# Linear attention and FFN on one core: reciprocals of the denominators taken by rows, split in two parts, and spread by products with a 0/1 matrix

## The reference

```python
q, k, v = phi(proj(Wq, bq)), phi(proj(Wk, bk)), proj(Wv, bv)     # phi = elu + 1
# chunks of 128 tokens, state (S, z) carried from one to the next
num  = mask(q k^T) v + q S
kcum = cumsum(k) + z
den  = sum(q * kcum, over the 16 features of a head)             # one number per token and head
out  = num / den
x = x + (out @ Wo.T + bo)
h = layernorm(x) * gamma + beta
x = x + 0.5 * (silu(h @ w1 + b1) @ w2 + b2)
```

## Time and profile before

| what | value |
|---|---|
| median of 3 runs | 1517.52 us (1516.9 to 1517.61) |
| the profiled execution's own time | 1522.6 us |
| its span, first to last instruction | 1520.8 us |
| mean granted TensorE clock | 0.991 |
| PE busy | 1493.2 us, 98% |
| DVE busy | 1283.5 us, 84% |
| ACT busy | 1129.7 us, 74% |
| POOL busy | 680.7 us, 45% |

### The profile page before, as it was taken

One profiled execution on the slowest core, in us unless ns is written; L12 is line 12 of the kernel. 1 busy time (PEld: TensorE's weight loads), 2 busy tenths in 40 slices (PEclk: granted clock), 3 DMA queues, 4 the chain that ended last, 5 costly groups with the idle time before them and its releaser, 6 DMA issues.

```text
span 1520.8 us, 40737 instructions
## 1 busy us (share of the span) xinstructions
PE 1493.2 (98%) x14874; PEld 1311.2 (86%) x14874; DVE 1283.5 (84%) x2587; ACT 1129.7 (74%) x1917; POOL 680.7 (45%) x469
## 2 busy tenths in 40 slices
PE   7799999999999999999999999999999999999998
PEld 6588889888888888888888888888888888988887
DVE  6788888888888888888888888888888888888875
ACT  3487777887777887777887777887777877777863
POOL 3244344544344544345444445443445443445444
PEclk8899999999999999999999999999999999999999
DMA  7846765556765556764557765557654557755450
GB/s 198 194 118 150 179 148 149 137 131 152 179 158 131 131 133 164 179 156 133 131 122 175 179 133 143 137 125 179 179 138 138 133 129 179 174 134 141 117 127 28
DMA packets 153944, 222.96 MB, mean 147 GB/s; under 512 B 20032, under 2 KB 71488, under 8 KB 153920
## 3 DMA queue, kind: packets, MB, share of 16 engines
q1 hardware_dynamic: 152560, 222.63, 61.0%
q10 hardware_dynamic: 1360, 0.01, 0.1%
HBM read 138.69 MB, written 83.89 MB: 146 GB/s over the span
## 4 chain that ended last, share of the span: by engine, by line
PE 93%; DVE 2%; DMA 2%; POOL 1%; issue 1%; SPq 0%; ACT 0%; POOLq 0%; DVEq 0%
PE ring L342 35%; PE num L532 8%; PE ring L420 8%; PE sc L490 7%; PE ring L421 7%; PE sc L342 6%; PE num L499 4%; PE num L342 3%; PE state_acc L342 3%; PE ring L372 3%; PE state_acc L490 2%; PE ring L566 2%; PE state_acc L513 2%; PE num L421 1%; PE num L420 1%; PE num L372 1%
## 5 line engine op out<-in xcount | busy, mean ns | idle before, releaser
L1137 POOL TENSOR_TENSOR s_lo<-silu_f,s_hi 128x512 fp32r<-128x512 f32 x256 | 343.9, 1349 | 539.0 <-ACT s_hi L987 538.9
L342 PE MATMUL ring<-w_hi,s_hi 128*128 128x256 f32 x992 | 282.2, 284 | 0.0
L342 PE MATMUL ring<-w_lo,s_hi 128*128 128x256 f32 x992 | 278.9, 281 | 0.0
L342 PE MATMUL ring<-w_hi,s_lo 128*128 128x256 f32 x992 | 278.9, 281 | 0.0
L672 DVE TENSOR_TENSOR probs<-sc,causal 128x512 f32<-128x512 f32 x320 | 207.6, 681 | 16.1 <-PE sc L490 8.6
L342 PEld LDWEIGHTS ring<-w_hi,s_hi 128*128 128x128 f32 x992 | 187.8, 189 | 12.1 <-DVE phi_q L718 12.0
L1032 ACT ACTIVATE x_hat<-x,hn_add,ln_rstd 128x256 f32<-128x256 f32 x128 | 66.5, 590 | 174.6 <-DVE hn_add L860 174.6
L976 ACT ACTIVATE silu_f<-ring,bias,scale 128x512 f32<-128x512 f32 x217 | 167.5, 772 | 31.9 <-PE ring L421 23.5
L420 PE MATMUL ring<-gt_hi,w_q 128*128 128x512 f32 x441 | 190.5, 432 | 0.0
L342 PEld LDWEIGHTS ring<-w_hi,s_lo 128*128 128x128 f32 x992 | 188.0, 189 | 0.0
L342 PEld LDWEIGHTS ring<-w_lo,s_hi 128*128 128x128 f32 x992 | 187.9, 189 | 0.0
(11 more groups left out here) (204 smaller groups left out, 3946.2 us busy)
## 6 DMA issues: line engine op xcount, KB each, us to landing
k_stack<-k_rows SPq DMA_DIRECT2D x192, 256.0 KB, 4.1
q_stack<-q_rows SPq DMA_DIRECT2D x384, 128.0 KB, 6.2
k_rows<-silu_f SPq DMA_DIRECT2D x128, 256.0 KB, 2.6
q_rows<-probs SPq DMA_DIRECT2D x128, 256.0 KB, 2.5
x_in<-in_x SPq DMA_DIRECT2D x32, 512.0 KB, 8.4
xb<-in_x SPq DMA_DIRECT2D x32, 512.0 KB, 7.9
out<-clip SPq DMA_DIRECT2D x64, 256.0 KB, 7.5
silu_f<-in_q SPq DMA_DIRECT2D x2, 512.0 KB, 10.4
```

The lines of the kernel that those rows point to most:

```text
L342: last = e.matmul(target, a, b, start=(n == 0), stop=(n == 3 * len(pairs) - 1))
L1137: sl.done(e.tensor_tensor(s_lo[:, j, :], silu_f[:, j % SLOTS, :], s_hi[:, j, :].bitcast(F32), ALU.subtract))
```

## The change

The denominators are now laid out so that a row of `num[1]` holds one head of one chunk: `head_one` has two variants of 32 columns, and for each of the four 32-row groups two fp32 products of 128 columns (chunk 2*half and 2*half+1) are summed into it. Every denominator stands in two rows. There is no copy out and no transpose back: VectorE takes one reciprocal of 128x128 straight from PSUM. ScalarE makes from it, in four operations of 128x128 with a factor of 0 or 1 per row (`row_kind`), the rounded part and the full value, GpSimd subtracts them (128x256) so that one of the two rows holds the rounded reciprocal and the other the remainder, and TensorE multiplies these by a 0/1 matrix `spread`, two float32r products of 256 columns with 64 rows per half t, in place of the four transposes. `values(3)` now stands ahead of `spread_reciprocals(0)`. VectorE's `residual` moves from the start of the iteration to behind `attention(1)`. GpSimd builds `row_kind` and `spread` once, at the start.

```diff
-                        last = e.matmul(num[1][32 * g:32 * g + 32, 0:2 * P], head_one[:, :],
-                                        qk[:, t, 2 * P * half:2 * P * (half + 1)], start=True, stop=True,
-                                        skip_group_check=True)
+                        for q in range(2):
+                            c = 2 * half + q
+                            last = e.matmul(num[1][32 * g:32 * g + 32, 0:P], head_one[:, q, :],
+                                            qk[:, t, c * P:(c + 1) * P], start=(q == 0), stop=(q == 1),
+                                            skip_group_check=True)
                 den_pe.done(last)
 
-            def denominators_back():
-                w.need(den_sb, 0)
-                for x in range(2):
-                    last = e.transpose(num[1][:, (2 + x) * P:(3 + x) * P], den_rows[:, x * P:(x + 1) * P], ident[:, :])
-                den_tr.done(last)
-
             def spread_reciprocals(t):
-                w.need(rspread, 0)
+                w.need(rden_made, 0)
                 free_bank(w, f"rb{t}", present)
-                for c in range(C):
-                    last = e.transpose(ring_bank(f"rb{t}")[:, c * P:(c + 1) * P],
-                                       qk[:, t, c * P:(c + 1) * P], ident[:, :])
+                rows = slice(t * 2 * 32, (t + 1) * 2 * 32)
+                for half in range(2):
+                    last = e.matmul(ring_bank(f"rb{t}")[:, half * 2 * P:(half + 1) * 2 * P],
+                                    spread[rows, half, :], rden_parts[rows, :, :].rearrange("p q n -> p (q n)"), start=True, stop=True)
                 rb_pe.done(last)
@@ order on TensorE
             fc1(3)
-            denominators_back()
             scores(3)
...
             from_state(2)
+            values(3)
             spread_reciprocals(0)
-            values(3)
@@ VectorE
             def reciprocals():
-                w.need(den_tr, 0)
-                for t in range(T):
-                    last = e.reciprocal(rden_tok[:, t, :, :].rearrange("p (a x) h -> p a x h", a=2), den_tok(t))
-                rden.done(last)
+                w.need(den_pe, 0)
+                rden.done(e.reciprocal(rden_full[:, 0, :], num[1][:, 0:P]))
...
             if Fn:
-                residual()
                 ffn_input_lo()
...
             attention(1)
+            if Fn:
+                residual()
@@ ScalarE, in place of denominators_out and reciprocals_spread
+            def reciprocals_low():
+                w.need(rden, 0)
+                for q in range(2):
+                    e.activation(rden_parts[:, q, :], rden_full[:, 0, :], ACT.Copy, scale=row_kind[:, 2 + q, 0:1])
+                for q in (1, 0):
+                    last = e.activation(rden_full[:, q, :], rden_full[:, 0, :], ACT.Copy, scale=row_kind[:, q, 0:1])
+                rden_low.done(last)
@@ GpSimd, ahead of ffn_lo(3)
+            def reciprocal_parts():
+                w.need(rden_low, 0)
+                rden_made.done(e.tensor_tensor(rden_parts[:, :, :], rden_full[:, :, :], rden_parts[:, :, :].bitcast(F32), ALU.subtract))
@@ GpSimd, once, behind the memset of v_pad: 15 operations, the longest of them
+                for n in range(T * 32 // HT):
+                    t, d = divmod(n, 32 // HT)
+                    e.wait_ge(p_spread, P_KIND + n)
+                    e.affine_select(out=ones_at, in_=ones_at, compare_op=ALU.not_equal, fill=1.0, base=-(64 * t + HT * d),
+                                    pattern=[[-32, 2], [-1, HT], [0, HD]], channel_multiplier=1).then_inc(p_spread, 1)
```

More of the change, by code:

```diff
@@ L142, in build @@
         probs = [sb(f"probs{n}", [P, HT, P]) for n in range(2)]
-        den_rows = sb("den_rows", [P, 2 * P])
+        rden_full = sb("rden_full", [P, 2, P])
+        rden_parts = sb("rden_parts", [P, 2, P], F32R)
+        spread = sb("spread", [P, 2, P], F32R)
+        row_kind = sb("row_kind", [P, 4, 4])
         gt_hi, gt_lo = sb("gt_hi", [P, T, S], F32R), sb("gt_lo", [P, T, S], F32R)
@@ L282, in build @@
         Waiter.idle = sem("idle")
+        p_spread = sem("p_spread")
         p_const, p_bias, p_dma = sem("p_const"), sem("p_bias"), sem("p_dma")
@@ L784, in reciprocals @@
             def reciprocals():
-                w.need(den_tr, 0)
-                for t in range(T):
-                    last = e.reciprocal(rden_tok[:, t, :, :].rearrange("p (a x) h -> p a x h", a=2), den_tok(t))
-                rden.done(last)
+                w.need(den_pe, 0)
+                if not Fn:
+                    e.wait_ge(p_spread, P_SPREAD)
+                rden.done(e.reciprocal(rden_full[:, 0, :], num[1][:, 0:P]))
             def attention(t):
@@ L1046, in keys_out @@
                                         ring_bank(f"kt{n}")[:, :].rearrange("p (c d) -> p c d", c=2), ACT.Copy))
[L1048 to L1052, removed]
+            def reciprocals_low():
                 w.need(rden, 0)
-                rspread.done(e.activation(qk[:, :, :].rearrange("p t (c h x) -> p (t c h) x", c=C, x=HD),
-                                          rden_tok[:, :, :, :].rearrange("p t c h -> p (t c h)")[:, :, None]
-                                          .to_broadcast([P, U * HT, HD]), ACT.Copy))
+                if not Fn:
+                    e.wait_ge(p_spread, P_SPREAD)
+                for q in range(2):
[3 more added lines that the diff above has]
+                rden_low.done(last)
             def reciprocals_out(t):
@@ L1090, in ac_iteration @@
             if A:
-                reciprocals_spread()
+                reciprocals_low()
             ffn_scaled(4)
@@ L1141, in po_iteration @@
             for j in range(2, FT):
+                if A and j == 3:
+                    reciprocal_parts()
                 if A and j == FT - 2:
@@ L1235, in build @@
         V_W1, V_BIAS_O, V_BETA, V_W2, V_BIAS_2 = 3, 4, 5, 6, 7
-        CONSTS = 6 + 6 + 1 + 1
+        CONSTS = 6 + 8 + 1 + 1
         def stage_of(n):
@@ L1331, in _, with reciprocal_rows @@
             po_norm(e, Waiter(e, -1), 1)
+            def reciprocal_rows(e):
+                kinds = row_kind[:, :, :].rearrange("p (k q) g -> p k q g", k=2)
+                ones_at = rden_full[:, :, :].rearrange("p a (h x) -> p a h x", x=HD)
+                e.memset(row_kind[:, :, :], 1.0).then_inc(p_spread, 1)
+                e.memset(rden_full[:, :, :], 0.0).then_inc(p_spread, 1)
+                e.wait_ge(p_spread, 2)
+                e.affine_select(out=kinds, in_=kinds, compare_op=ALU.is_ge, fill=0.0, base=0,
+                                pattern=[[-HT, 2], [-2 * HT, 2], [-32, 4]], channel_multiplier=1).then_inc(p_spread, 1)
+                e.wait_ge(p_spread, 3)
+                e.affine_select(out=kinds, in_=kinds, compare_op=ALU.is_ge, fill=0.0, base=2 * HT - 1,
+                                pattern=[[0, 2], [2 * HT, 2], [32, 4]], channel_multiplier=-1).then_inc(p_spread, 1)
+                e.wait_ge(p_spread, 4)
+                e.tensor_tensor(row_kind[:, :, 0:2], row_kind[:, :, 0:2], row_kind[:, :, 2:4], ALU.add).then_inc(p_spread, 1)
+                e.wait_ge(p_spread, 5)
+                e.tensor_tensor(row_kind[:, :, 0:1], row_kind[:, :, 0:1], row_kind[:, :, 1:2], ALU.add).then_inc(p_spread, 1)
+                for n in range(T * 32 // HT):
[3 more added lines that the diff above has]
+                                    pattern=[[-32, 2], [-1, HT], [0, HD]], channel_multiplier=1).then_inc(p_spread, 1)
+                e.wait_ge(p_spread, P_SPREAD - 1)
+                e.tensor_tensor(spread[:, :, :], rden_full[:, :, :], rden_full[:, :, :], ALU.mult).then_inc(p_spread, 1)
             e.wait_ge(xhat.sem, xhat.value(0, 0))
             e.memset(v_pad[:, :, :, :, :], 0.0).then_inc(p_const, 1)
+            reciprocal_rows(e)
             po_iteration(e, -1, False, False, True, True)
```

20 lines of the change are left out of this document (11 added, 9 removed).

## The result

| | before | after |
|---|---|---|
| median | 1517.21 us (6 runs, 1514.79 to 1519.65) | 1526.87 us (6 runs, 1524.47 to 1530.74) |
| ratio | | 1.0070, 95% interval 1.0057 to 1.0082 |
| profiled execution: span | 1520.8 us | 1525.8 us |

What follows compares the result with a forecast made beforehand. TensorE was taken to bound the kernel (93% of the chain). Profiled: 1522.6 + 1.2 (0.04 us over 31 batches) + 0.5 at the start = 1524.3 us; median 1517.5 + 1.7, say 1519; range 1507 to 1530, forecast's own 1515 to 1524.

Steps and rivals of the forecast that it cites:

- the places of the ties: Between denominators and fc1(7), TensorE is tied to others at three places: fc1(3)'s weight load, mask(2) before scores(3), ffn_sum(6) before fc1(7).
- the hidden operand chain: Reciprocals through VectorE, ScalarE and GpSimd: operand ready at 734.8, needed by TensorE at 735.3, so hidden with 0.5 us of room.
- rival 2: Column groups of denominators fall in line instead of side by side: slower, 1526 to 1536 us, strict order 1546; chance 0.15.
- Two prices, 0.12 and 0.20 us, and a 64-row product switches the mode: On TensorE, 0.12 us into narrow products, 0.20 out; the 64-row spreads assumed to cost 0.20 in and 0.20 out.
- rival 1: The 64-row spreading products need no mode switch: 0.29 us a batch faster, 1509 us; chance 0.30.
- `denominators` side by side: Four 32-row groups still run in parallel on TensorE with 8 products of 128 columns: 0.44 against 0.44 us, no change.
- Rival 3: The spread's operand reaches TensorE late, after values(3): 0.25 us a batch, 1526 us; chance 0.05.
- The transposes' removal, 0.09: Dropping the two L558 transposes lets scores(3) stream earlier on TensorE, limited by mask(2): gain 0.09 us.
- Nearest is the middle ... 0.5 us, nothing changes: VectorE's one 128x128 reciprocal, between 0.24 and 0.96 us, taken as 0.5 against 0.48 before; at 0.96, 0.2 us a batch lost.
- The later one counts: 0.04 us later than before: Second half of fc1(7): VectorE's side ready at 740.66, TensorE's at 740.79, so 0.04 us a batch longer, +1.2 us over 31.
- Once, at the start, 0.5: Eight GpSimd selections of 128x256 beside VectorE's weight splits cost 0.5 us once, bounds 0 to 2.
- `residual` hidden by `phi_k`: Moved residual fills VectorE's idle 1.45 us before phi_k, ending 0.13 late, absorbed by phi_q's 0.49 of idle; decides over 2 us.

Runs made afterwards that it cites:

- e1: Changed kernel with the 0/1 spread matrix given all 128 rows (zeros outside the wanted token half); ratio 1.0006 to the kernel before.
- b_no_back: Kernel before without the two transposes that bring the denominators back, attention left undivided; ratio 0.9982 to the kernel before.
- e4: Changed kernel with the reciprocal taken of only 32 of the 128 columns (result partly wrong); ratio 1.0020 to the kernel before.
- e3: Changed kernel with only VectorE's residual moved back to the start of its iteration; ratio 1.0040 to the kernel before.
- e5: Changed kernel with VectorE's attention(0) moved behind ffn_sum(6); ratio 1.0072 to the kernel before.
- before_again: Kernel before, unedited, run again for a second trace; its execution took 1519.46 us, with batches of 45.64 us.
- e6: Changed kernel with the full-height (128-row) spread and attention(0) behind ffn_sum(6); ratio 1.0016 to the kernel before.
- e7: Changed kernel with full-height spread, attention(0) behind ffn_sum(6), and each half's second spreading product split into two of 128 columns; ratio 1.0043 to the kernel before.
- e9: Changed kernel with full-height spread, attention(0) behind mask(6), and shared buffers at the kernel before's SBUF addresses; ratio 1.0047 to the kernel before.
- b_attention_later: Kernel before with only attention(0) moved behind ffn_sum(6) on VectorE; ratio 1.0040 to the kernel before.
- the second comparison: The changed kernel, unedited, timed again beside the kernel before; ratio 1.0086 (1.0071 to 1.0101).

## Why the prediction was right and wrong

The prices of the switches, the places of the ties and the hidden operand chain were right. The forecast itself, 1.7 us slower with a range of its own of 1515 to 1524, was not: 9.7 us were lost. That 1526.9 lies in the stated range of 1507 to 1530 is luck, since the part above 1524 was put there for rival 2, which didn't come true.

- *Two prices, 0.12 and 0.20 us, and a 64-row product switches the mode* (forecast against rival 1): right. Both spreads show it, and e1, which differs in the height of the tile, gets 0.24 us back. Rival 1 is out.
- *`denominators` side by side* (against rival 2): right, 0.66 against 0.61 us. Rival 3 is out as well: 0.7 us of room.
- *The transposes' removal, 0.09*: right; `scores(3)` streams 0.11 us earlier in the batch than in before, of which 0.03 were there at `fc1(3)` already, and b_no_back has 0.09 at the end of the stretch.
- *"Nearest is the middle ... 0.5 us, nothing changes"*: the first step that failed. The reciprocal takes 0.87 us of VectorE's time, 0.39 more than the pair before; its length grows with its columns (348 ns for 32 in e4, 946 for 128). The free time that the prediction counted ahead of `fc1(4)`, some 0.3 us, was about right, and 0.39 is 0.1 more than that. It cost just the lead won at the transposes: `fc1(4)` streams 0.01 us later than in before, not 0.09 earlier. The prediction had 0.96 as upper bound, and 0.2 us a batch for it.
- *"The later one counts: 0.04 us later than before"*: the term that was mis-sized. TensorE's own side counted with that lead of 0.09. Without it the 0.04 are 0.13, and with the 0.07 of wait in `scores(6)` (e3, e5) they are 0.20. The traces show 0.20 and 0.19 in the median.
- *The long run of products*: not in the prediction at all. It took the "even distance" as given. 119.0 instead of 118.15 ns over 132 products is 0.11 us a batch, a third of the loss.
- *Once, at the start, 0.5*: the first key product starts at 14.31 us, in before_again at 13.69:
```profile
13.69 0.47 PE L342 MATMUL ring<-xt_hi,wk_hi 128*128 128x512 f32 x1 [1.81 <-DVE xt_lo L704]
```
```profile
14.31 0.47 PE L344 MATMUL ring<-xt_hi,wk_hi 128*128 128x512 f32 x1 [2.10 <-DVE xt_lo L703]
```
  All four traces without the change have 13.63 to 13.69, those with it 13.99 to 14.53. The eight selections aren't the cause: they begin at 14.08 on GpSimd, 0.6 us after VectorE began on that product's last operand. What is ahead are two more selections for `head_one`: GpSimd's first power of the norm starts at 8.16 instead of 7.84. That is half of the 0.6; the other half wasn't traced. By the first `fc2` the mean lies 2.5 us later (107.5 to 114.7 in ten traces with the change, 106.4 to 111.6 in four without), but this goes with TensorE's granted clock, whose mean over the first 106 us is 0.82 to 0.90. The three traces with the change that have 0.87 there (e4, e6, e7) reach the first `fc2` at 108.3 to 109.2, and before, with 0.87 as well, at 109.2; at 0.89 it is 107.5 in e9 and 106.6 in b_attention_later. So a loss of 2.5 us isn't shown. Whether the change alters the clock there is open.
- *`residual` hidden by `phi_k`*: right in its place (it ends as `phi_k` starts), but not free: e3 has 0.06 us a batch through `attention(0)`, and 0.96 us in iteration 31, where there is no `phi_k` to hide behind. The prediction put both at nothing; it read one batch in the middle and not the last one with attention.

Sum: 0.20 to 0.22 in the stretch (medians and means) and 0.11 in the run, times 30, are 9.3 to 9.9 us; with 1.0 in iteration 31 and 0.6 at the start that is 10.9 to 11.5. To be taken off are 0.6 us that before loses once, in both its traces, ahead of `scores(4)` in iteration 30, and no other kernel does, for a reason that wasn't traced. That leaves 10.3 to 10.9, against 9.7 (8.6 to 12.4 by the interval) and 13 (10.8 to 15.3) in the second comparison. The losses in the stretch and in iteration 31 are shown by edits. That the pace goes with the addresses is likely, and not shown by itself. For it: nine traces at the new addresses have 119.0, whatever was edited, and none of the five at the old ones does, e9 among them. Against taking it as shown: e9 also has `attention(0)` behind `mask(6)`, a place that no kernel at the new addresses has, and TensorE stands still for 0.48 us right ahead of its run; and b_attention_later shows that at the old addresses the order on VectorE can shift the pace. Which address it would be, and what picks one of three paces at the old ones, is open; an edit of before with nothing but the new addresses was not tried.

## What to carry to other kernels

Price a change in the height of a tile before you take it: zeros up to the full height were cheaper here than two switches of 0.20 us around two products of 0.12. When several small terms meet at a tie, work out each side again with the pessimistic value of every term: the lead of 0.09 us was gone after one operation of 0.87 instead of 0.5. When an operation is moved into an idle place, look whether that place is idle in the first and the last iteration too: here one that isn't cost 1.0 us. And compare traces of several executions of the kernel before, at a stretch that the change doesn't touch, before a difference of 0.5% is put down to the change's instructions.

## What the runs showed of the hardware

- Back-to-back float32r products of 256 columns have no single cost: on average 117.3, 118.7 or 120.0 ns from start to start with one layout of SBUF (before, b_attention_later, e9) and 118.2 with another (after), all at full granted clock. One of these averages holds through a run of 132.
- Two products of 256 columns from a tile of 64 rows cost 0.20 us to get into and 0.20 to get out of between full-height ones, and nothing more than themselves, 0.24 us, when the tile had 128 rows (e1).
- A VectorE reciprocal of fp32 costs about 0.2 us for each 32 columns: 317 ns at 32, 946 at 128.
- VectorE's scaling of the residual took 1.75 us in the changed kernel and 3.33 beside GpSimd's subtractions. ScalarE's copies of 128x128 took 386 ns each and started 0.29 us apart, which is the 0.3 that the prediction allowed.
